# Rows kept unscaled between attention layers, and the targets' diagonal made on ScalarE

## What is computed

```python
def _gat_layer(x, src, dst, ea, W, We, a_s, a_d, a_e, b, g, beta):
    h = x @ W
    e = ea @ We
    alpha = h @ a_s
    alpha = alpha[src] + (h @ a_d)[dst] + e @ a_e
    alpha = jax.nn.leaky_relu(alpha, NEG_SLOPE)
    alpha = _segment_softmax(alpha, dst, N)
    out = jax.ops.segment_sum(h[src] * alpha[:, None], dst, num_segments=N) + b
    mu = out.mean(-1, keepdims=True)
    var = ((out - mu) ** 2).mean(-1, keepdims=True)
    return (out - mu) * jax.lax.rsqrt(var + LN_EPS) * g + beta
```

## Time and profile before

| what | value |
|---|---|
| median of 3 runs | 2232.75 us (2230.29 to 2233.54) |
| the profiled execution's own time | 2236.65 us |
| span of its instructions | 2234.9 us |
| PE, PEld busy | 1663.9 us (74%), 1239.8 us (55%) |
| DVE busy | 1751.1 us (78%) |
| ACT busy | 1496.0 us (67%) |
| POOL busy | 1154.6 us (52%) |
| mean granted TensorE clock | 0.867 of full |

### The profile page before, as it was taken

How to read it: one execution, slowest core, us unless ns; L and a number is a source line. 1 busy time by engine, 2 the same in 40 slices (tenths; PEclk the granted TensorE clock), 3 DMA queues, 4 the chain that set the end, 5 groups by cost and what they waited for, 6 DMA issues and landing times. The chain is left out here.

```text
span 2234.9 us, 41269 instructions
## 1 busy us (share of the span) xinstructions
PE 1663.9 (74%) x9595; PEld 1239.8 (55%) x9595; DVE 1751.1 (78%) x8774; ACT 1496.0 (67%) x7686; POOL 1154.6 (52%) x1069
## 2 busy tenths in 40 slices
PE   2589388888488885884996884996884996984980
PEld 1589255555277773552884552884552884542760
DVE  3680599999489995895996895996995996895870
ACT  0352299999389994992765992765992765992540
POOL 0477777400045555774225774225774225773777
PEclk9995599999689996996996996996996996995985
DMA  8013323321312123113113113113113113124321
GB/s 144 21 39 97 94 66 98 87 59 43 84 36 66 53 69 78 43 47 84 37 58 88 43 47 84 36 60 86 43 47 84 36 60 87 43 47 107 90 75 35
DMA packets 123138, 145.21 MB, mean 65 GB/s; under 512 B 56197, under 2 KB 83637, under 8 KB 122145
## 3 DMA queue, kind: packets, MB, share of 16 engines
q1 hardware_dynamic: 66303, 116.40, 19.1%
q0 software_dynamic: 56160, 25.40, 5.7%
q10 hardware_dynamic: 432, 0.79, 0.1%
HBM read 94.60 MB, written 67.86 MB: 73 GB/s over the span
## 5 line engine op out<-in xcount | busy, mean ns | idle before, releaser
L212 POOL DMA_INDIRECT S<-row_t,rowI x400 | 540.3, 1351 | 224.0 <-issue 224.0
L944 PE MATMUL bank<-AC,XT 128*125 128x390 f32 x800 | 330.5, 519 | 0.3
L1008 ACT ACTIVATE R<-bank 125x128 f32<-125x128 f32 x1200 | 323.2, 308 | 0.0
L1008 ACT ACTIVATION_READ_ACCUMULATOR R<-bank 125x1 f32 x1200 | 278.5, 242 | 0.0
L1663 POOL TENSOR_TENSOR R<-ident,aselfS 125x250 f32<-125x250 f32 x150 | 95.3, 637 | 333.7 <-PE bank L1691 257.8
L200 PEld LDWEIGHTS bank<-ident,Y 125*128 125x128 f32 x800 | 98.4, 150 | 215.3 <-issue 150.3
L200 PE MATMUL bank<-ident,Y 125*128 125x125 f32 x800 | 131.3, 290 | 115.2 <-ACT XT L992 52.0
L1710 PE MATMUL bank<-WCX,XT 128*125 128x130 f32 (+1 forms) x1400 | 210.2, 289 | 2.6 <-ACT XT L1739 2.4
L1739 ACT ACTIVATE XT<-bank 128x250 f32<-128x250 f32 x200 | 76.0, 380 | 190.6 <-PE bank L1691 182.4
L1689 PE MATMUL bank<-R,S 125*128 125x125 f32 x800 | 174.3, 300 | 33.9 <-DVE R L1779 27.6
L1050 DVE BATCH_NORM_STATS2 st<-R 125x6 f32<-125x128 f32 x800 | 173.0, 278 | 31.5 <-issue 31.1
(11 more groups left out here) (425 smaller groups left out, 5122.1 us busy)
## 6 DMA issues: line engine op xcount, KB each, us to landing
row_t<-T SPq DMA_DIRECT2D x40, 568.8 KB
R<-in_x SPq DMA_DIRECT2D x100, 224.0 KB
out_rows<-R SPq DMA_DIRECT2D x100, 224.0 KB
R<-m_t SPq DMA_DIRECT2D x5, 2734.4 KB
S<-row_t,rowI POOLq DMA_INDIRECT x400
T<-in_edge_attr SPq DMA_DIRECT2D x1, 5600.0 KB
x_t<-XB SPq DMA_DIRECT2D x50, 112.0 KB
R<-x_t SPq DMA_DIRECT2D x25, 224.0 KB
```

The costliest lines, as they stand in the source:

```text
L212: pool.indirect_dma_start(to, None, table, bass.IndirectOffsetOnAxis(ap=idx, axis=0), bounds_check=rows - 1, oob_is_err=False).then_inc(do ...
L944: nc.tensor.matmul(LAYERS[a][0:P, 0:3 * D + 6], h0(g, a), ACB[:, 0:3 * D + 6], start=True, stop=True).then_inc(layers_done.s, 1)
L1008: ins = nc.scalar.activation(JUNK[:, a * 3 + l, :], LAYERS[a][0:P, l * D:(l + 1) * D], ACT.Square, scale=D ** -0.5, accum_out=NRM[:, g % N ...
```

## The change

A row of `S` and `T` gets a 131st number (`RW = W + 1`), the mean of its squares. Layers 0 to 2 no longer divide: `root`, `invert`, `rescale_t` and `rescale_s` are gone there, and ScalarE writes the mean square into the new column. The next layer's softmax block takes the roots and inverses for all columns at once (`rrS`, `rrT`), scales the scores by them, and multiplies them into `alphaS`, `aselfS` and `DG`; `add_bias_s` multiplies by `rrS`. The diagonal of layers 0 to 2 moves from GpSimd to ScalarE. The lags on TensorE, ScalarE and VectorE are new; on ScalarE also those of the last layer. The crossing chain of layers 0 to 2 ends with a copy and a square.

```diff
+RW = W + 1
-        S = sb("S", [P, C, W])
-        T = sb("T", [P, TC, W])
+        S = sb("S", [P, C, RW])
+        T = sb("T", [P, TC, RW])
-        row_t = nc.dram_tensor("row_t", [P * TC, W], F32, kind="Internal").ap()
+        row_t = nc.dram_tensor("row_t", [P * TC, RW], F32, kind="Internal").ap()
+                nc.vector.memset(S[:, :, W:RW], 1.0)
+                nc.vector.memset(T[:, :, W:RW], 1.0)
...
+                    if l:
+                        dve.wait_ge(*rooted.at(1))
+                        ch.add(nc.vector.reciprocal(sx[:, 1:2], sx[:, 0:1]))
+                        ch.link(nc.vector.reciprocal(rrT[:, :], rrT[:, :]))
+                        nc.vector.tensor_scalar(sx[:, 3:5], T[0:C, C, D:W], sx[:, 1:2], None, ALU.mult)
+                        nc.vector.tensor_tensor(scT[:, :, :], T[:, 0:C, D:W],
+                                                rrT[:, :].unsqueeze(2).broadcast_to([P, C, 2]),
+                                                ALU.mult).then_inc(scored.s, 1)
+                        dve.wait_ge(*rooted.at(2))
+                        ch.link(nc.vector.reciprocal(rrS[:, :], rrS[:, :]))
+                        nc.vector.tensor_tensor(scS[:, :], S[:, :, D], rrS[:, :], ALU.mult).then_inc(scored.s, 1)
                     dve.wait_ge(*columns_in.at(1))
...
-                    nc.vector.tensor_copy(alphaS[:, :], banks[0][0:P, 0:C])
-                    nc.vector.tensor_copy(aselfS[:, :], banks[0][0:P, C:2 * C])
+                    if l:
+                        nc.vector.tensor_tensor(alphaS[:, :], banks[0][0:P, 0:C], rrS[:, :], ALU.mult)
+                        nc.vector.tensor_tensor(aselfS[:, :], banks[0][0:P, C:2 * C], rrT[:, :], ALU.mult)
...
+                    if l:
+                        pe.wait_ge(*scored.at(1))
+                    nc.tensor.transpose(banks[1][0:C, 0:P], own, ident[0:P, 0:P])
+                    nc.tensor.transpose(banks[2][0:C, 0:P], target, ident[0:P, 0:P])
+                    if l:
+                        pe.wait_ge(*scored.at(2))
+                    nc.tensor.transpose(banks[0][0:C, 0:P], source, ident[0:P, 0:P]).then_inc(columns_in.s, 1)
...
+                    if l:
+                        nc.scalar.activation(rrT[:, :], T[:, 0:C, W], ACT.Sqrt, bias=epsc[:, 0:1])
+                        nc.scalar.activation(sx[:, 0:1], T[0:C, C, W:RW], ACT.Sqrt,
+                                             bias=epsc[0:C, 0:1]).then_inc(rooted.s, 1)
+                        nc.scalar.activation(rrS[:, :], S[:, :, W], ACT.Sqrt, bias=epsc[:, 0:1]).then_inc(rooted.s, 1)
...
-                        run_slot(t, NU, [(5, put)] if final else [(0, diagonal)])
+                    if final:
+                        for t in slots:
+                            run_slot(t, NU, [(5, put)])
...
-                        run_slot(t, NU, [(0, aggregate), (1, multiply_t)] if final else [(4, multiply_s), (4, multiply_t), (3, aggregate), (0, turn)])
+                        run_slot(t, NU, [(0, aggregate), (1, multiply_t)] if final else [(1, turn), (3, multiply_s), (2, aggregate), (3, multiply_t)])
...
+                    def diagonal(n):
+                        if n >= NS:
+                            act.wait_ge(*gathered.at(n - NS + 1))
+                        for a in range(2):
+                            ins = nc.scalar.activation(DGB[:, n % NS, a, :], ident[0:P, 0:P], ACT.Copy,
+                                                       scale=aselfS[:, 2 * n + a:2 * n + a + 1])
+                        ins.then_inc(diag_ready.s, 1)
...
                         for a in range(2):
+                            ins = nc.scalar.activation(Y[:, r, a, :], T[:, 2 * n + a, 0:D], ACT.Square, scale=D ** -0.5,
+                                                       accum_out=T[:, 2 * n + a, W:RW])
+                        ins.then_inc(t_ready.s, 1)
+                        act.wait_ge(*bias_s.at(n + 1))
+                        for a in range(2):
+                            nc.scalar.activation(Y[:, r, 2 + a, :], S[:, 2 * n + a, 0:D], ACT.Square, scale=D ** -0.5,
+                                                 accum_out=S[:, 2 * n + a, W:RW])
...
-                        run_slot(t, NU, [(4, squares), (2, copy_t), (4, root)])
+                        run_slot(t, NU, [(3, root), (1, copy_t), (2, squares)] if final else [(4, squares), (2, copy_t), (0, diagonal)])
...
+                        for a in range(2):
+                            z = product(banks[4 + n % NS], 2 * P)[:, a, :]
+                            if l:
+                                ins = nc.vector.scalar_tensor_tensor(S[:, 2 * n + a, 0:W], z, rrS[:, 2 * n + a:2 * n + a + 1],
+                                                                     BB[:, l, :], ALU.mult, ALU.add)
+                            else:
+                                ins = nc.vector.tensor_tensor(S[:, 2 * n + a, 0:W], z, BB[:, l, :], ALU.add)
...
-                        run_slot(t, NU, [(0, diagonal), (0, mask), (4, rescale_t), (3, invert), (1, edge)] if final else [(0, mask), (1, add_bias_s), (0, copy_s), (1, add_bias_t), (2, edge), (3, invert), (5, rescale_t), (3, rescale_s)])
+                        run_slot(t, NU, [(0, diagonal), (0, mask), (4, rescale_t), (3, invert), (1, edge)] if final else [(0, mask), (2, add_bias_t), (1, add_bias_s), (0, copy_s), (4, edge)])
...
+                    if not final:
+                        dve.wait_ge(*x_pe.at(3))
+                        stage(nc.vector.tensor_copy(T[0:C, C, 0:W], banks[2][0:C, 0:W]), 3)
+                        return
```

More of the change, by code:

```diff
@@ L137, in gnn_kernel @@
         rowI = stream("rowI", I32)
-        alphaS, aselfS, repNS, DS, WIS = (stream(n) for n in ("alphaS", "aselfS", "repNS", "DS", "WIS"))
+        alphaS, aselfS, repNS, DS, WIS, rrS, rrT, scS = (stream(n) for n in (
+            "alphaS", "aselfS", "repNS", "DS", "WIS", "rrS", "rrT", "scS"))
+        scT = sb("scT", [P, C, 2])
         AE = sb("AE", [C, L, P])
@@ L1621, in attention @@
                 s.base += 1
+            for s in (rooted, scored):
+                s.base += 2 if l else 0
             bias_t, bias_s = signal("addend_added", "score_kept")
             (masked, diag_ready, gathered, agg_copied, edged, agg_done, turned, turned_copied, next_done, squared,
-             rooted, inverted, t_ready, s_ready, scaled, x_stage, x_act, x_pe) = signal(
+             rooted, inverted, t_ready, scaled, x_stage, x_act, x_pe) = signal(
                 "masked", "diagonal_ready", "aggregated", "turned1_copied", "edge_columns_kept", "conv_done",
                 "turned2", "turned2_copied", "score_ready", "counted1", "root1", "inverse1", "t_rows_ready",
-                "s_rows_ready", "scale1", "crossing_vector", "crossing_scalar", "crossing_tensor")
+                "scale1", "crossing_vector", "crossing_scalar", "crossing_tensor")
             slots = range(NU + 5)
@@ L1744, in squares @@
                             act.wait_ge(*agg_done.at(n + 1))
-                        else:
-                            act.wait_ge(*bias_t.at(n + 1))
-                        for a in range(2):
-                            v = product(banks[r], 2 * P)[:, a, 0:D] if final else T[:, 2 * n + a, 0:D]
-                            ins = nc.scalar.activation(Y[:, r, a, :], v, ACT.Square, scale=D ** -0.5,
-                                                       accum_out=ss4[:, r, a:a + 1])
-                        if not final:
-                            act.wait_ge(*bias_s.at(n + 1))
-                            for a in range(2):
-                                ins = nc.scalar.activation(Y[:, r, 2 + a, :], S[:, 2 * n + a, 0:D], ACT.Square,
-                                                           scale=D ** -0.5, accum_out=ss4[:, r, 2 + a:3 + a])
@@ L1821, in rescale_t @@
                         dve.wait_ge(*inverted.at(n + 1))
-                        if final:
-                            for a in range(2):
-                                ins = nc.vector.scalar_tensor_tensor(
-                                    T[:, 2 * n + a, 0:D], product(banks[r], 2 * P)[:, a, :], rr4[:, r, a:a + 1], G3[:, :],
-                                    ALU.mult, ALU.mult)
-                            ins.then_inc(scaled.s, 1)
-                            dve.wait_ge(*scaled.at(n + 1))
-                            dve.wait_ge(x1_loaded[n // 2 % 5], 32 * (n // 10 + 1))
-                            f0 = 2 * n % 20
-                            nc.vector.tensor_tensor(T[:, 2 * n:2 * n + 2, 0:D], T[:, 2 * n:2 * n + 2, 0:D],
-                                                    XF[:, f0:f0 + 2, :], ALU.add).then_inc(t_ready.s, 1)
-                            return
@@ L1834, in rescale_t @@
-                        nc.vector.tensor_tensor(T[:, 2 * n:2 * n + 2, :], T[:, 2 * n:2 * n + 2, :],
-                                                rr4[:, r, 0:2].unsqueeze(2).broadcast_to([P, 2, W]),
```

(11 more changed lines are left out.)

83 lines of the change are left out of this document (46 added, 37 removed).

## The result

| kernel | median, us | runs | ratio to the kernel before, 95% interval |
|---|---|---|---|
| before | 2232.85 (2230.29 to 2233.54) | 4 | |
| changed | 2151.11 (2148.81 to 2153.95) | 4 | 0.9637 (0.9620 to 0.9653) |

What follows compares the result with a forecast made beforehand. VectorE was taken to bound the layer blocks, TensorE after the change. -73.5 (layer blocks) + 7.8 (softmax) - 0.9 (last layer) = -66.6 us, from 2236.65 to 2170.0; the runs' median stands 3.9 lower: 2166, range 2157 to 2194.

Steps and rivals of the forecast that it cites:

- The crossing chain: End of each of layers 0 to 2: a copy and a square replace four instructions, 0.4 us less.
- ScalarE's sum: ScalarE's work per unit after the change: 2.02 us, with the diagonal's two copies overlapping at 0.59.
- new wait: Rival: a new wait replaces the old, 2.44 us a unit through the long ring, 2220 us; chance 0.07.
- the clock: Rival: TensorE's clock falls in the layer blocks; at a third of the units 2266 us; chance 0.03.
- TensorE's own floor: TensorE's shortest unit in the layer blocks, read from an early unit of the kernel before: 2.07 us.
- 21.4: Layer block from its first multiply_t to the last multiply_t's loads: 122.2 us becomes 100.8, 21.4 less.
- The rival in which ScalarE is the bound: Layer blocks: the diagonal's copies do not overlap, so ScalarE's unit is 2.20 us; total 2185 us; chance 0.2.
- The tail: Each layer block, from the last multiply_t's loads to the crossing transpose: 4.29 us becomes about 1.6, 2.7 less.
- The softmax block: Layers 1 to 3: first transposes wait for roots and inverses, 2.6 us more per block, bounds 1.5 and 4.
- the 0.9 forecast: Last layer: first scatter about 0.9 us earlier, and with it GpSimd's chain of scatters that ends the kernel.
- -73.5: Change in us for three layer blocks together, 24.5 less per layer.
- +7.8: Change in us for the softmax blocks of layers 1 to 3 together, 2.6 more each.

Runs made afterwards that it cites:

- e1: Changed kernel with multiply_t(n) put right after multiply_s(n) on TensorE in layers 0 to 2; 2161.1 us.
- e2: Changed kernel with both multiplies side by side on TensorE, but multiply_t, add_bias_t, edge and squares one unit later; 2168.1 us.
- e5: Changed kernel with turn transposing one source tile instead of two, so half of the source products use stale numbers; 2148.1 us (one run).
- e14: Changed kernel with six more squares on ScalarE, for which TensorE waits before the crossing transpose of layers 0 to 2; 2157.1 us (one run).
- e13: Changed kernel with targets' root before the crossing square, inverse after the crossing copy, crossing transpose awaiting the last addition, sources' scores scaled before small reciprocal; 2139.9 us.
- e6: Kernel before with only the diagonal of layers 0 to 2 moved from GpSimd to ScalarE, all rescaling kept; 2190.0 us.
- e10: Kernel before, unchanged, run and profiled once more; 2232.2 us.
- e9: Kernel before with rows of 131 numbers instead of 130, the last never used; 2232.7 us.
- e3: Changed kernel with the diagonal of layers 0 to 2 back on GpSimd as one instruction; 2154.7 us.

## Why the prediction was right and where it was wrong

**Right:** the mechanism. VectorE held the pace, GpSimd's diagonal stretched it, and the block then ran at TensorE's sum, with no idle time before its loads. ScalarE's sum was forecast as 2.02 and is 2.00; the diagonal's copies overlap. No new wait came, and in the middle of the blocks the clock stays at 1.00.

**The step that failed:** "So TensorE's own floor is 2.07 us at full clock". TensorE's floor is 2.00. The early unit of the earlier trace rows had no wait for VectorE, but it had one for ScalarE's copy_t, 0.08 us in the middle of a row that groups eight loads: the fifth load starts at 1062.36, not 1062.28. e1 brings the wait back and e2 takes it away. The working had even said that the new lags give copy_t a whole group, and didn't take the time off. From first to last aggregate the block lost 24.8 us (123.8 to 99.0) where the forecast had 21.4; 49 x 0.07 is 3.4. Over the three layers it is 74.0 against 64.2, 10 us. The rival in which ScalarE is the bound is half true: it is full as well, at the same 2.00 (e5), and not at 2.20.

**The tail.** From the end of the last loads to the crossing transpose 4.29 us became 1.63, 2.7 less, as forecast (from the last aggregate on it is 6.4 and 4.1, 2.3 less). The crossing chain was mis-sized: 0.4 forecast, 1.5 measured. The fewer instructions gave 0.5 to 0.6; the rest, about 1.0, is TensorE coming to the chain at its upper clock (e14), which the forecast did not ask about, although have PE at 0.44 us for a transpose. This term was 3.3 us too small over the three layers. The first aggregate also comes 0.3 us earlier in each block (1.1 to 0.8 us after the first mask).

**The softmax block.** 2.9 us a block, where 2.6 was forecast with bounds of 1.5 and 4. About half of it can be had back by other placing alone (e13).

**The last layer.** In the first pair of profiles the first scatter comes 10.9 us after the block's start and not 12.1. But this place varies without any change: with the old last layer it is 12.1, 11.5, 11.5 and 10.8 (before, e6, e10, e9), with the new one 10.6 to 11.2 (12 profiles). The block takes 174.0 to 175.0 us with the old one, 174.4 on average, and 172.4 to 174.3 with the new one, 173.4 on average. That fits the 0.9 forecast, but the first pair alone (174.1 and 174.3) shows nothing of it.

**Outside the blocks** nothing was forecast. About 4 us of the 82 are there. Such differences also show between executions of one kernel, so they are not shown to be of the change, nor shown not to be.

In sum: -73.5 was -86.2 for the layer blocks, +7.8 was +8.6. The 12.7 us between the first two are 10 from the unit, 3.3 from the crossing chain and 0.9 from the start, less 1.2 since the stretch up to the last aggregate is counted to another mark than the forecast's. The range took 1 to 2 us a layer for the tail and nothing for the unit: it had a bound above for TensorE's sum and none below.

## What to carry to other kernels

A unit that doesn't wait for the engine you relieve may still hold a short wait for a third; before it is taken for an engine's floor, add up the distances between its single instructions, and see whether each group of equal loads takes the same time wherever it stands (here 0.96 against 1.04 us for eight). When work moves into a tail, what ends the stage decides: a table load of 1.28 us was free ahead of a hand-over and cost 1.3 behind it. Where two parts of a change relieve the same engine (here 42 and 80 us by themselves, 82 together), the second should be costed against a kernel that has the first.

## What the runs showed of the hardware

- A full ScalarE has longer durations at the same pace. In the changed kernel a square shows 0.37 us and its accumulator read 0.26; in e1, where ScalarE has 0.07 us to spare in each unit, 0.30 and 0.19 (e6, full again: 0.36 and 0.26). The distances from start to start are 0.29 in all. Durations alone would put the changed unit's squares at 4 x 0.63 = 2.5 us, longer than the unit.
- TensorE's granted clock after a gap: over the crossing chain it was 0.95 behind 1.43 us of idle time (changed kernel) and 0.51 behind 4.46 us (e14); the same chain took 3.33 and 4.36 us.
- The mask, which has a bf16 operand, is stretched beside a GpSimd instruction as rescale_s was: 0.41 to 0.83 us (e3).
